# Graph attention on one core: two of four heads' maxima moved from a stage of their own into the main loop

## The reference, cut to what matters

```python
z = jnp.einsum('ni,hif->nhf', h, W)
el = jnp.einsum('nhf,hf->nh', z, a_l)
er = jnp.einsum('nhf,hf->nh', z, a_r)
e = jax.nn.leaky_relu(el[src] + er[dst], NEG_SLOPE)
m = jax.ops.segment_max(e, dst, num_segments=N)
ex = jnp.exp(e - m[dst])
s = jax.ops.segment_sum(ex, dst, num_segments=N)
alpha = ex / s[dst]
out = jax.ops.segment_sum(alpha[:, :, None] * z[src], dst, num_segments=N)
```

## Time and profile before

| | |
|---|---|
| time, median of 3 executions | 2593.78 us (2592.81 to 2595.72) |
| the profiled execution: span from the first to the last instruction | 2589.7 us |
| PE busy | 2465.5 us, 95% of the span |
| DVE busy | 1968.1 us, 76% |
| ACT busy | 1230.4 us, 48% |
| mean granted TensorE clock | 0.978 |
| attention: first maximum to last matmul of the main loop | 270.8 to 502.5 us |

### The profile page before, as it was taken

The page is one execution under the profiler, slowest core; times in us unless marked ns, Lnnn a source line. Parts: engine busy times, 40 slices in busy tenths (PEclk is TensorE's granted clock), DMA queues, the critical chain, the costliest instruction groups (busy, mean ns, idle before and its releaser), DMA issues. The chain is left out here.

```text
span 2589.7 us, 34729 instructions
## 1 busy us (share of the span) xinstructions
PE 2465.5 (95%) x12652; PEld 1666.1 (64%) x12652; DVE 1968.1 (76%) x2504; ACT 1230.4 (48%) x1413; POOL 143.8 (6%) x173
## 2 busy tenths in 40 slices
PE   6999299889999999999999999999999989999998
PEld 4666287756666666666666666666666556568776
DVE  7876799798888897797797788788788756665422
ACT  6322676565555455445545545545544235522111
POOL 1000000010000000000000000000000011000222
PEclk9999699989999999999999999999999999999999
DMA  5211311143232232322421422422331045836993
GB/s 164 63 39 39 67 40 40 67 141 62 73 63 57 75 61 57 88 49 55 95 57 41 96 56 41 96 56 47 88 105 49 1 136 178 264 135 211 353 379 109
DMA packets 145389, 252.12 MB, mean 97 GB/s; under 512 B 67128, under 2 KB 82106, under 8 KB 138838
## 3 DMA queue, kind: packets, MB, share of 16 engines
q1 hardware_dynamic: 135378, 231.40, 31.3%
q0 software_dynamic: 4928, 10.25, 1.6%
q10 hardware_dynamic: 4932, 8.30, 0.9%
HBM read 204.01 MB, written 49.33 MB: 98 GB/s over the span
## 5 line engine op out<-in xcount | busy, mean ns | idle before, releaser
L1761 PE MATMUL wide_ps<-keep_own_room,rails_hid_hi 128*125 128x512 f16 x4200 | 1250.7, 379 | 5.2 <-DVE rails_hid_lo L1478 3.2
L1761 PE MATMUL wide_ps<-keep_own_room,rails_hid_lo 128*125 128x512 f16 x2100 | 796.4, 379 | 0.0
L1761 PEld LDWEIGHTS wide_ps<-keep_own_room,rails_hid_hi 128*125 128x125 f16 x4200 | 564.7, 137 | 312.5 <-issue 6.4
L1761 PEld LDWEIGHTS wide_ps<-keep_own_room,rails_hid_lo 128*125 128x125 f16 x2100 | 286.9, 137 | 167.0 <-issue 0.6
L1253 ACT ACTIVATE rails_hid_hi<-rails_raw_a,keep_scale_hidden 128x1000 f16<-128x1000 f32 x210 | 274.5, 1334 | 209.5 <-DVE rails_raw_a L1497 90.8
L1478 DVE SCALAR_TENSOR_TENSOR rails_hid_lo<-rails_raw_a,keep_scale_hidden,rails_hid_hi 128x1000 f16<-128x1000 f32 x210 | 312.1, 1516 | 41.7 <-ACT rails_hid_hi L1253 41.6
L1243 ACT ACTIVATE rails_raw_a<-wide_ps,keep_scale_gelu 128x1000 f32<-128x1000 f32 (+1 forms) x192 | 181.6, 951 | 323.6 <-PE wide_ps L1746 320.2
L1532 DVE SCALAR_TENSOR_TENSOR keep_X<-wide_ps,rails_out_scale,keep_X 125x1024 f32<-125x1024 f32 x180 | 198.6, 1103 | 132.3 <-PE wide_ps L1761 132.3
L1486 DVE SCALAR_TENSOR_TENSOR keep_own_room<-carried_w_land,rails_w_scale,keep_own_room 128x2048 f16<-128x2048 f32 x105 | 246.0, 2343 | 0.7 <-ACT keep_own_room L1268 0.7
L1268 ACT ACTIVATE keep_own_room<-carried_w_land,rails_w_scale 128x2048 f16<-128x2048 f32 x105 | 208.9, 1990 | 9.8 <-DVE carried_w_land L1516 5.7
L1228 ACT ACTIVATE rails_raw_a<-carried_w_land 128x2048 f32<-128x2048 f32 x64 | 121.7, 1902 | 141.9 <-DMA carried_w_land<-cproj 141.7
(11 more groups left out here) (476 smaller groups left out, 3359.3 us busy)
## 6 DMA issues: line engine op xcount, KB each, us to landing
carried_w_land<-cproj SPq DMA_DIRECT2D x79, 1024.0 KB
ffn_w_up<-split_d SPq DMA_DIRECT2D x9, 2048.0 KB
keep_own_room<-W SPq DMA_DIRECT2D x11, 1024.0 KB, 5.8
ffn_w<-W SPq DMA_DIRECT2D x11, 1024.0 KB
rails_xs<-xt_d SPq DMA_DIRECT2D x124, 78.1 KB
keep_comb_hi<-W SPq DMA_DIRECT2D x8, 1024.0 KB, 7.2
split_d<-graph_high SPq DMA_DIRECT2D x16, 512.0 KB, 6.6
keep_X<-split_d SPq DMA_DIRECT2D x4, 2048.0 KB
```

Source lines behind the costliest of these rows:

```text
L1761: mm = nc.tensor.matmul(ps[0:P, t, :], hid[(q + b) % 2][l][:, k, t * P:(t + 1) * P], w[(q + b) % 2][r][:, k, :], start=(k == 0 and i == 0) ...
```

## The change

Head 1 alone keeps its maxima in the first block beside head 0; heads 2 and 3 have theirs in the main loop. The first block so has 20 maxima with 20 masks, and the loop has 20 with 20. The column terms of heads 1, 2 and 3 are each made, turned, copied, stored and spread by themselves: in DVE's steps 2, 24 and 46, ahead of PE's steps 3, 26 and 48, and at the end of ACT's steps 4, 27 and 49. In the first block the columns of head 0 follow maximum 11 instead of 16, the copies of rows stand behind masks 9, 11 and 12, and the copies of `el` for heads 2 and 3 behind all masks.

```diff
-        LATE_MAX = {2 + 9 * t // 2: t for t in range(TILES)}
-        LATE_COLS, LATE_LINES = SWITCH - 6, SWITCH - 4
-        ps_line, ps_last = ps[0:2 * (HEADS - 2) * TILES, 6, :], ps[0:2 * TILES, 2, :]
-        maxima = [(t, t, 0) for t in range(TILES)] + [(TILES + t, t, h) for t in range(TILES) for h in range(1, LAST)]
-        maxima += [(2 * TILES + t, t, LAST) for t in range(TILES)]
-        EARLY = LAST * TILES
-        FIRST_COLS = TILES + 6
+        LATE_MAX = {3 + 11 * t // 5: t for t in range(TILES)}
+        LATE_MAX.update({26 + 2 * t: TILES + t for t in range(TILES)})
+        COLS_AT, LINES_AT, LINES_BY = {2: 1, 24: 2, 46: 3}, {3: 1, 26: 2, 48: 3}, {TILES: 1, 3 * TILES: 2, SWITCH: 3}
+        ps_line = [ps[0:2 * TILES, bank_of, :] for bank_of in (6, 1, 2)]
+        maxima = [(h * TILES + t, t, h) for h in range(HEADS) for t in range(TILES)]
+        EARLY = 2 * TILES
+        FIRST_COLS = TILES + 1
...
         def mask(act, m):
             if m >= 2:
-                act.wait_ge(maxed, used_masks(m - 2))
+                act.wait_ge(maxed, m - 1)
...
                 for m in range(1, 2 * TILES):
                     mask(act, m)
-                    if m in (7, 9, 10):
-                        take_rows({7: 1, 9: 2, 10: 3}[m], row_a, {7: 1, 9: 2, 10: 3}[m])
-                    if m == TILES + 4:
-                        take_rows(HEADS, row_a, 0)
-                    if m == TILES + 6:
-                        take_rows(HEADS + 1, row_b, 0)
+                    if m == TILES - 1:
+                        take_rows(1, row_a, 1)
+                    if m == TILES + 1:
+                        take_rows(2, row_a, 0)
+                    if m == TILES + 2:
+                        take_rows(3, row_b, 0)
+                for h in range(2, HEADS):
+                    take_rows(h + 2, row_a, h)
                 nc.scalar.activation(warm[:], far[:], ACT.Exp, scale=-1.0)
...
-                for h in range(HEADS):
+                for h in range(2):
                     spread(h, el, h)
                 pe.wait_ge(cols_set, 4)
-                spread(HEADS, col_a, 0)
-                spread(HEADS + 1, col_b, 0)
+                spread(2, col_a, 0)
+                spread(3, col_b, 0)
+                for h in range(2, HEADS):
+                    spread(h + 2, el, h)
...
                 def rows_back(h):
+                    sp.wait_ge(lines_set[h - 1], 1)
+                    sp.dma_start(rows_d[2 * h * TILES:2 * (h + 1) * TILES], lines[h - 1][:]).then_inc(lines_out[h - 1], 16)
+                    sp.wait_ge(lines_out[h - 1], 16)
                     sp.dma_start(row_a[:, h, :], by_row[h, 0].partition_broadcast(P)).then_inc(rows_in[h], 16)
...
-                    if m == 2:
-                        columns_of(dve, 1, LAST, 4)
+                    if m in COLS_AT:
+                        h = COLS_AT[m]
+                        dve.wait_ge(maxed, (h + 1) * TILES)
+                        columns_of(dve, h, h + 1, 4 * h)
                     if m in LATE_MAX:
                         maximum(dve, EARLY + LATE_MAX[m])
-                    if m == LATE_COLS:
-                        dve.wait_ge(maxed, HEADS * TILES)
-                        columns_of(dve, LAST, HEADS, 8)
...
                     if m + 1 in LATE_MAX:
-                        mask(act, 2 * TILES + LATE_MAX[m + 1])
-                    if m == LATE_LINES + 1:
-                        act.wait_ge(last_turned, 1)
-                        nc.scalar.copy(last_lines[:], ps_last[:, 0:P]).then_inc(last_set, 1)
-                    if m == 6:
-                        act.wait_ge(lines_turned, 1)
-                        nc.scalar.copy(lines[:], ps_line[:, 0:P]).then_inc(lines_set, 1)
+                        mask(act, EARLY + LATE_MAX[m + 1])
+                    if m - 1 in LINES_AT:
+                        h = LINES_AT[m - 1]
+                        act.wait_ge(lines_turned[h - 1], 1)
+                        nc.scalar.copy(lines[h - 1][:], ps_line[h - 1][:, 0:P]).then_inc(lines_set[h - 1], 1)
...
-                    if m == 3:
-                        pe.wait_ge(cols_set, 8)
-                        nc.tensor.transpose(ps_line[:, 0:P], cols[:, 1:LAST].rearrange("p h k t -> p (h k t)"),
-                                            ident[0:P, 0:P]).then_inc(lines_turned, 1)
-                    if m == LATE_LINES:
-                        pe.wait_ge(cols_set, 12)
-                        pe.wait_ge(taken, 4 * HALF_T)
-                        nc.tensor.transpose(ps_last[:, 0:P], cols[:, LAST].rearrange("p k t -> p (k t)"), ident[0:P, 0:P]).then_inc(last_turned, 1)
+                    if m in LINES_AT:
+                        of = LINES_AT[m]
+                        pe.wait_ge(cols_set, 4 * (of + 1))
+                        if of >= 2:
+                            pe.wait_ge(taken, (2 * HALF_T, 4 * HALF_T)[of - 2])
+                        nc.tensor.transpose(ps_line[of - 1][:, 0:P], cols[:, of].rearrange("p k t -> p (k t)"),
+                                            ident[0:P, 0:P]).then_inc(lines_turned[of - 1], 1)
+                    if m in LINES_BY:
+                        pe.wait_ge(lines_set[LINES_BY[m] - 1], 1)
```

More of the change, by code:

```diff
@@ L659, in attention @@
         col_a, col_b = [cols[:, :, k].rearrange("p h t -> p t h") for k in range(2)]
-        lines, last_lines = c.sb("lines", [2 * (HEADS - 2) * TILES, P], F32), c.sb("last_lines", [2 * TILES, P], F32)
-        lines_turned, lines_set, lines_out = c.sem("lines_turned"), c.sem("lines_set"), c.sem("lines_out")
-        last_turned, last_set, last_out = c.sem("last_turned"), c.sem("last_set"), c.sem("last_out")
+        lines = [c.sb(f"lines{h}", [2 * TILES, P], F32) for h in range(1, HEADS)]
+        lines_turned, lines_set = [c.sem(f"lines_turned{h}") for h in range(1, HEADS)], [c.sem(f"lines_set{h}") for h in range(1, HEADS)]
+        lines_out = [c.sem(f"lines_out{h}") for h in range(1, HEADS)]
         warm, first_cells = c.sb("warm", [P, 1], F32), c.sb("first_cells", [P, HALF], F32)
@@ L696, in maximum @@
             dve.wait_ge(edgeless, m + 1)
-            dve.wait_ge(rows_set, h + 1)
+            dve.wait_ge(rows_set, (1, 2, 5, 6)[h])
             to = n % 2 if n < EARLY else 0
@@ L822, in _ @@
             def _(sp):
-                sp.wait_ge(lines_set, 1)
-                sp.dma_start(rows_d[2 * TILES:2 * LAST * TILES], lines[:]).then_inc(lines_out, 16)
-                sp.wait_ge(lines_out, 16)
                 by_row = rows_d.rearrange("(h k t) p -> h k (t p)", h=HEADS, k=2)
                 def rows_back(h):
+                    sp.wait_ge(lines_set[h - 1], 1)
+                    sp.dma_start(rows_d[2 * h * TILES:2 * (h + 1) * TILES], lines[h - 1][:]).then_inc(lines_out[h - 1], 16)
+                    sp.wait_ge(lines_out[h - 1], 16)
                     sp.dma_start(row_a[:, h, :], by_row[h, 0].partition_broadcast(P)).then_inc(rows_in[h], 16)
@@ L834, in rows_back @@
                     sp.dma_start(row_b[:, h, :], by_row[h, 1].partition_broadcast(P)).then_inc(rows_in[h], 16)
-                for h in range(1, LAST):
+                for h in range(1, HEADS):
                     rows_back(h)
[L838 to L841, removed]
                 rows_to(sp, zh[:, LAST, :, 0:HEAD_F], z_d.rearrange("(t p) (h f) -> p h t f", p=P, h=HEADS)[:, LAST], z_in[LAST])
@@ L967, in _ @@
                         pe.wait_ge(z_in[h], 32)
-                    if m == 3:
-                        pe.wait_ge(cols_set, 8)
-                        nc.tensor.transpose(ps_line[:, 0:P], cols[:, 1:LAST].rearrange("p h k t -> p (h k t)"),
-                                            ident[0:P, 0:P]).then_inc(lines_turned, 1)
-                    if m == LATE_LINES:
-                        pe.wait_ge(cols_set, 12)
-                        pe.wait_ge(taken, 4 * HALF_T)
-                        nc.tensor.transpose(ps_last[:, 0:P], cols[:, LAST].rearrange("p k t -> p (k t)"), ident[0:P, 0:P]).then_inc(last_turned, 1)
-                    if m == SWITCH:
-                        pe.wait_ge(last_set, 1)
+                    if m in LINES_AT:
[7 more added lines that the diff above has]
+                        pe.wait_ge(lines_set[LINES_BY[m] - 1], 1)
                     if m == LAST * 2 * TILES:
                         pe.wait_ge(ones_set, 2)
-                    if m == TILES:
-                        pe.wait_ge(lines_set, 1)
                     pe.wait_ge(wt_set, m + 1)
```

## The result

The changed kernel takes 2602.28 us (median of 6, 2601.26 to 2604.43), the kernel before beside it 2593.72 us (median of 6): a ratio of 1.0032, with a 95% interval of 1.0021 to 1.0044. It is slower by 8.6 us; 2603.8 was predicted. The span of the profiled execution is 2599.4 us, 9.7 above the one before. One of the twelve executions of the run with lines turned earlier took 3296.66 us at a mean granted clock of 0.745; the median given for that run, 2597.15 us, counts it (2596.86 without it), its ratio does not.

The account below looks back on a forecast made before the run. DVE was taken to bound the first block and, narrowly, the loop up to the fifth `take`, then PE. Loop loss 15.7, first-block gain 7.0 and clock 1.3 gave +10.0: span 2599.7, median 2603.8 us, range 2596 to 2609.

Parts of the forecast that it names:

- The first block: Ten fewer maxima, 13.8 us by themselves, were to gain 7.0 us after waits, with bounds of 5 and 12.
- the walk: Step-by-step count of the first block: DVE idle 5 us for mask 12, ACT last, loop starting at about 310.0.
- The rival that the block doesn't stall: First block, no stall at mask 12: gain 12.1 us, so +4.9 in all, 2598.7 us; chance 0.06.
- The loop: From the loop's start to the fifth `take`: 136.1 us instead of 120.4, a loss of 15.7 us.
- DVE's small idle time: Half-microsecond waits for ACT in blocks one to three, 1.5, 1.3 and 0.6 us before; taken as 0, upper bound 4 us.
- The same prices: DVE's costs in the loop: a step 1.50 us, a maximum 1.38, a statistics instruction 0.60, a `take` 2.38.
- the loop hides the maxima: Rival: DVE's work fits behind the matmuls, so only the first block's 7.0 us counts, 2586.8 us; chance 0.07.
- the waits at the copies are covered: Rival: ACT is further ahead, sparing 3.5 + 3.8 + 2.1 us; loop loss 6.3, no clock loss, 2593.1 us; chance 0.09.
- The clock: PE's gaps of 4.0 us may lower its clock; 1.3 us counted, for blocks two and four, bounds 0 and 4.8.
- SP and the loads: One more small store and the row and head loads in the loop were to cost nothing.
- The 4.1 us from span to median: The median time was taken as 4.1 us above the profiled span, turning 2599.7 into 2603.8 us.
- the fourth: Rival: the clock falls in every gap and the first block gains only 5: +15.5, 2609.3 us; chance 0.13.

Follow-up runs that it names:

- the run with lines turned earlier: Against the changed kernel, PE turns the lines of heads 1, 2, 3 ahead of its steps 1, 24, 46 instead of 3, 26, 48: 2597.15 us.
- the masks ahead: Against the changed kernel, ACT copies head 0's two column rows behind masks 14 and 17 instead of 11 and 12: 2600.17 us.
- the kernel before with the like edits: The kernel before, with head 3's columns turned earlier, their copy later, and ten statistics instructions moved behind the fifth `take`: 2589.01 us.
- both edits: The changed kernel with lines turned ahead of PE's steps 1, 24, 46 and head 0's column rows copied behind masks 14 and 17: 2591.48 us.
- the run with the late statistics: The changed kernel with earlier line turns, later column-row copies, and ten statistics instructions moved to steps 54 to 58 and 64 to 68: 2585.20 us.

## Why the prediction was right

**The first block.** Predicted gain 7.0 us, measured 7.1. Each stall of the walk is there with its size: 1.0 us at mask 10, 5.0 at mask 12, 1.0 at mask 13, and ACT as the last engine. The rival that the block doesn't stall is out; taking the stall away by another order gave 4.3 us.

**The loop.** Predicted loss 15.7, measured 15.9; no block is off by more than 0.05 us, and the start by 0.3, most of it because PE's first 30 records took 9.22 us instead of the 8.99 counted. DVE's small idle time, for which I had left up to 4 us, was nothing: between the `take`s DVE waited at the copies only. The same prices had missed blocks of the kernel before by up to 1.5 us, so 0.05 is closer than they could promise. The rivals "the loop hides the maxima" and "the waits at the copies are covered" are out: without head 3's maxima the third block fell to PE's floor, and with earlier turns the idle times of 3.60 and 3.62 us vanished and the one of 2.00 fell to 0.62. Blocks one to four hold eight more maxima than before, 11.0 us, and are 11.4 us longer together: the idle time of the kernel before beyond the prices (3.4 us in blocks one to three) went, and the new wait of 3.6 us at the copy in block two came. Of these 3.4 us the prediction calls all waits for a mask; 0.75 in block one was a wait for PE.

**The clock** is the term that was mis-sized for this profile: I counted 1.3 us, and it cost nothing. PE waited 3.62 and 3.73 us, and the windows of the changed kernel behind the longest wait show full clock:

```profile
418.00:422.00 4.00, 0.39 (x2) 0.00 (x0) 3.93 (x11) 3.66 (x5) 0.00 (x0) 1.00 0.00 0
422.00:425.00 3.00, 2.88 (x13) 2.49 (x14) 3.00 (x7) 0.56 (x1) 0.00 (x0) 1.00 0.02 5
```

It isn't a wrong mechanism, though: behind the same wait of 3.73 us the clock was 0.50 in the run with early turns. Where the code of the loop is the same, the same wait went either way: 2.96 us kept the clock in the changed kernel and 2.97 didn't with the masks ahead, and neither did 3.61 us there, where 3.62 kept it. What decides it stays open, and the sum from one profile can't know it. The Trainium skill, page "TensorE: Matmul & The Clock Gate", section "HAM oscillation — how this bites in real kernels", tells of a kernel whose TensorE waits between its groups of matmuls and starts every one of them cold; by these traces some groups do, and none of the changed kernel's behind a `take` did. What it costs depends on the place. In blocks one and three a slow PE has room, or nearly: with the masks ahead block one was 0.3 us longer and block three the same. In block two it delays the turn of the lines and with it DVE, by 1.7 us in the run without head 3's maxima. For block four of the changed kernel this is argued only.

**SP and the loads** cost nothing, as argued: no wait stands in the 64.08 us behind the fifth `take`.

**The sum.** +10.0 predicted; without the clock term +8.7, and the medians differ by 8.6. The agreement of the last two is closer than the scatter allows one to claim, since the piece behind the fifth `take` moves by over 3 us between executions. The span hit, 2599.7 predicted and 2599.4 measured, is partly luck too: the two stages gave +8.8, and the 1.3 for the clock that didn't come was made up by 0.9 of scatter in front of and behind them. The 4.1 us from span to median was 2.9 here. And the prediction's range didn't only leave out the first two rivals: the fourth, at 2609.3, lies above its upper end of 2609.

What stays open is how often the clock falls in the changed kernel itself; its six times (2601.3 to 2604.4) would allow for some executions with a fall and some without: the two slowest, both 2604.43 us, have the lowest mean granted clock (0.977), the other four 0.979 or 0.980. But only one of the six has a trace.

## What to carry to other kernels

When two engines are both busy over 90% in a loop, find the points where one must wait for the other and price the work between them one block at a time: work that moves into a block whose length its own engine already sets costs its full time there. That can still pay: with the waits and the statistics out of the way the same split of the maxima was 3.5 us faster than the kernel before with the like edits. Look at what stands behind each waiting instruction in its engine's queue: here a copy of 0.25 us, which nothing needed for many microseconds, held up ACT by up to 3.96 us and DVE by up to 3.62, and turning its input two steps earlier gave back 7.1 us in the profile, as much as the first block had gained from ten maxima less. Work that has a late deadline (the statistics) belongs where the other engine sets the pace.

## What the runs showed of the hardware

TensorE's granted clock fell to 0.50 (1.2 GHz) behind waits of 3.73 us (early turns, and both edits) and, in the run with the masks ahead, of 2.97 and 3.61 us. It was at 0.56 in 360.5 to 363.5 behind a wait of 2.44 us in the run with the late statistics. In the run with both edits it stood at 0.52 in the first 2.7 us behind a wait of 1.93 us, with full clock in the window of the wait itself. The changed kernel kept 1.00 behind waits of 2.96, 2.44, 3.62 and 3.73 us. So the length of the wait alone doesn't decide it. The windows behind the 3.61 us (masks ahead), and those of the run with both edits:

```profile
391.30:394.00 2.70, 2.70 (x6) 2.16 (x7) 2.70 (x6) 0.37 (x1) 0.00 (x0) 0.50 0.00 0
```

```profile
333.00:335.30 2.30, 0.38 (x2) 0.00 (x0) 2.23 (x6) 2.30 (x3) 0.00 (x0) 1.00 0.01 4
335.30:338.00 2.70, 2.69 (x7) 2.12 (x8) 2.70 (x6) 1.30 (x3) 0.00 (x0) 0.52 0.00 0
```
